# Window attention's product with V: four 32-key groups per head pair replaced by one 64-key group on V and a shifted copy of V

## The chip, the cores and the metric

The kernel runs on one core of a Trainium2 chip. The metric is the device time of one launch in microseconds (us), the median of the runs. Lower is better.

## The reference

The input is 8 sequences of 512 tokens with 128 features. A first layer (linear attention with Taylor features, 16 heads) and a feed-forward transformer of 6 layers follow one another, each with a residual. The change touches the 6 layers only, in the attention over windows. Cut to what matters, for each of 6 layers:

```python
WINDOW, HEADS, DIM_HEAD = 32, 16, 64
qkv = x @ Wqkv                              # 128 -> 3 * 1024
q, k = l2norm(q) * qs, l2norm(k) * ksc      # per head
q = q * cos * scale + rotate_half(q) * sin * scale
k = k * cos * inv + rotate_half(k) * sin * inv
bk2, bv2 = look(bk), look(bv)               # window before + own window: 64 keys for 32 queries
sim = einsum('bhwie,bhwje->bhwij', bq, bk2) * 8
attn = softmax(where(mask, -max, sim), -1)  # 32 x 64 per window and head
out = einsum('bhwij,bhwje->bhwie', attn, bv2)
x = out.reshape(b, n, 1024) @ Wo + x
x = (a * gelu(gate)) @ W2 + b2 + x          # feed-forward, hidden width 341
```

So each block of 32 queries attends to the 64 keys of its own window and the one before it; the first window has no window before it.

## The kernel before

The features stand on the partitions (x is held transposed, 128 x 512 per sequence). A unit u is one sequence in one layer (48 units). A step n is one pair of heads of one unit (8 steps per unit, 384 in all, `NS`); an index m is two steps, that is four heads (192 in all), and the softmax works on one m at a time, in tiles of 128 x 1024.

Every engine runs its own list of stages. All lists come from one table, `PLACE`: stage `X` of step n (or of unit u, with 8u) is put at the place n + PLACE[X], the stages of all steps are sorted by place, and each engine issues its own ones in that order. A place therefore gives the order on an engine; it is no time. Semaphores hold the data dependences across engines. The stages are software-pipelined: the projection of step n stands about 7 steps ahead of its scores, the product with V some 4 steps behind.

The stages in the order in which a head pair goes through them, with lines of the profile (most matmuls are recorded at line 480, the helper `mm`, and are told apart by their tiles):

- PJ (TensorE, `PS<-LH,LXH` and `PS<-LXH,LH` rows are products of this kind, each as three products of high and low parts), PQ (ScalarE, L1177, squares into SX), PT (VectorE, L891: the two rotary products at once, into TPB), TS (SyncE, L445: TPB with neighbouring partitions swapped into TR by DMA), SS (TensorE, `PS<-SX,C`: sums of squares), AD (GpSimd, L1312: TPB + TR into Q or K).
- NM1, NM2, RW, RQ, RB: the inverse norms, by VectorE and ScalarE, written to DRAM (L453) and read back to all partitions as RB (SyncE, L463). PR (GpSimd, L1294) multiplies K by RB.
- S1 (TensorE): the mask product and then 64 small products `PS<-K,Q`, each a 64-row, 32-column piece of the array. It waits for PR of its second step.
- MX (VectorE, L915 and L920), S3 (ScalarE, L1201: 16 exponentials of 128 x 64 into SC), SU (VectorE, L926, L928), NP (GpSimd, L1317: probabilities times 1/sum).
- TT (VectorE, L936, L937): 32 x 32 block transposes; the part for the own window goes to PP[:, 0], that for the window before to PX. PX (SyncE, L470, L471): two DMAs move PX by 32 partitions into PP[:, 1], so that each block of 32 keys has beside it the probabilities of its own queries and of the queries of the next window.
- VP (TensorE) and VC (ScalarE, L1191): V of one 128-token chunk for eight heads, into VV.
- PV (TensorE, `PS<-PP,VV`): for each m four groups of 16 products (rho = 0 to 3). A product has 32 keys on 32 rows of the array, 64 columns of V, and 64 query columns (own and next window) as the moving operand; neighbouring key blocks add into the same PSUM columns, and so rho = 1 to 3 each wait until the group before is done (`pv_pe`). The four groups stand at four places in TensorE's list.
- PVn (ScalarE, L1214): 128 x 1024 from PSUM to AOT. WO and the feed-forward (F1 to F5) follow once per unit.

```python
PLACE = {
    "S1": 0.07, "MX": 0.18, "S3": (0.52, 0.62, 1.38, 1.44), "SU": 1.45, "NP": 1.74, "TT": 2.63, "PX": 2.78,
    "PV": (3.60, 3.67, 4.87, 5.14), "PVn": 5.23, "PJ": (-7.60, -7.06), "PQ": (-7.54, -7.13),
```

A float32 product appears as two MATMUL and two LDWEIGHTS records, so 64 products per m are 128 records, and 192 m make the count of 24576 in the rows.

## Time and profile before

| | |
|---|---|
| median of 3 runs | 3836.64 us (3830.94 to 3848.4) |
| profiled execution | 3838.31 us, its span 3836.5 us |
| TensorE busy | 3549.6 us (93%) |
| VectorE busy | 2627.8 us (68%) |
| ScalarE busy | 2549.0 us (66%) |
| GpSimd busy | 2022.4 us (53%) |
| mean granted TensorE clock | 0.980 |

Busy time is the time in which at least one instruction of the engine ran; since matmuls overlap, TensorE's busy time also counts the tails of small products. Idle time of an engine is put down to whatever released it. The first 670 us or so belong to the first layer, which the change only reorders; the rest is the 6 layers in a steady rhythm.

### The profile page before, as it was taken

To read this page: it belongs to the slowest core of one execution; us is meant where nothing else is said; L and a number is where in the kernel's file an instruction comes from. 1 tells how busy PE (TensorE), PEld (TensorE's weight loads), DVE (VectorE), ACT (ScalarE), POOL (GpSimd) and SP (SyncE) were. 2 spreads that over 40 slices of the span, in tenths; PEclk is the share of its full clock that TensorE was granted. 3 is DMA by queue.
4 is the path that set the end of the run, shared out by engine and by line. 5 is a ranking of instruction groups with operands and counts; after the bars stand their busy time and mean duration, and the time that the engine had idled before them with its cause. 6 is when DMAs were issued, how large, how long until landed. Compare 5 with 4: busy or idle time off the path is not lost.

```text
span 3836.5 us, 149435 instructions
## 1 busy us (share of the span) xinstructions
PE 3549.6 (93%) x65224; PEld 2293.5 (60%) x65416; DVE 2627.8 (68%) x3583; ACT 2549.0 (66%) x5965; POOL 2022.4 (53%) x1564
## 2 busy tenths in 40 slices
PE   7999998799999999999999999999999999999997
PEld 4555554466666666666666666666666666666664
DVE  3555555577777777777776777777777777767662
ACT  4655564476767676777666766777767767677773
POOL 0000000666666666666666666666666666666651
PEclk9999999799999999999999999999999999999997
DMA  1000000333333333333333433333433333433330
GB/s 49 6 6 6 6 6 3 130 129 117 123 125 132 121 124 121 122 130 129 118 121 114 138 123 123 115 124 121 136 117 128 113 132 120 134 113 126 126 109 25
DMA packets 222618, 389.72 MB, mean 102 GB/s; under 512 B 63758, under 2 KB 101900, under 8 KB 221836
## 3 DMA queue, kind: packets, MB, share of 16 engines
q1 hardware_dynamic: 196080, 364.42, 27.5%
q10 hardware_dynamic: 25884, 15.73, 1.4%
q8 instruction: 514, 8.42, 0.9%
q14 instruction: 140, 1.15, 0.1%
HBM read 124.14 MB, written 7.34 MB: 34 GB/s over the span
## 4 chain that ended last, share of the span: by engine, by line
PE 69%; DVE 12%; ACT 7%; issue 5%; DMA 3%; SPq 2%; POOL 1%; ACTq 0%; POOLq 0%; DVEq 0%
PE PS L480 68%; ACT SC L1201 4%; DVE MX L915 2%; DMA RB<-root_scratch 2%; DVE TPB L891 2%; DVE SM L926 2%; DVE PX L937 1%; DMA PP<-PX 1%; POOL K L1294 1%; DVE VAR L958 1%; ACT AOT L1214 1%; DVE H L965 1%; ACT XCH L1072 1%; DVE VAR L956 1%; DVE BQ L920 1%
## 5 line engine op out<-in xcount | busy, mean ns | idle before, releaser
L891 DVE SCALAR_TENSOR_TENSOR TPB<-PS,VEC,C 128x1024 f32<-128x1024 f32 x768 | 961.0, 1263 | 98.4 <-ACT SX L1177 89.2
L1201 ACT ACTIVATE SC<-PS,BQ,RQ 128x64 f32<-128x64 f32 x3072 | 966.2, 430 | 26.0 <-DVE BQ L920 25.6
L1294 POOL TENSOR_TENSOR K<-K,RB 128x512 f32<-128x512 f32 x384 | 492.4, 1282 | 727.2 <-DMA RB<-root_scratch 726.7
L480 PEld LDWEIGHTS PS<-PP,VV 32*64 32x64 f32 x24576 | 436.1, 133 | 314.0 <-issue 210.8
L480 PE MATMUL PS<-PP,VV 32*64 32x64 f32 (+1 forms) x24576 | 542.0, 223 | 72.1 <-ACT AOT L1214 32.9
L1177 ACT ACTIVATE SX<-PS 128x512 f32<-128x512 f32 x768 | 475.5, 628 | 195.0 <-PE PS L480 188.8
L926 DVE TENSOR_REDUCE SM<-SC 128x16 f32<-128x1024 f32 x192 | 234.2, 1220 | 388.7 <-ACT SC L1201 388.6
L1312 POOL TENSOR_TENSOR K<-TPB,TR 128x512 f32<-128x512 f32 x384 | 493.8, 1286 | 0.0
L1312 POOL TENSOR_TENSOR Q<-TPB,TR 128x512 f32<-128x512 f32 x384 | 492.9, 1284 | 0.0
L1317 POOL TENSOR_TENSOR SC<-SC,RC 128x1024 f32<-128x1024 f32 x192 | 366.2, 1907 | 158.1 <-DVE RC L928 154.5
L480 PE MATMUL PS<-LXH,LH 128*128 128x512 f32 x768 | 350.2, 456 | 16.9 <-DVE TPB L891 9.8
L1191 ACT COPY VV<-PS 128x512 f32<-128x512 f32 x384 | 238.3, 620 | 188.6 <-PE PS L480 185.5
L1214 ACT COPY AOT<-PS 128x1024 f32<-128x1024 f32 x192 | 197.3, 1028 | 248.0 <-PE PS L480 246.1
L480 PE MATMUL PS<-AOT,LO 128*128 128x512 f32 x768 | 338.6, 594 | 0.0
L480 PEld LDWEIGHTS PS<-K,Q 64*32 64x32 f32 x24576 | 255.8, 105 | 126.2 <-issue 80.5
L480 PE MATMUL PS<-K,Q 64*32 64x64 f32 (+1 forms) x24576 | 294.1, 225 | 35.0 <-issue 19.4
L480 PE MATMUL PS<-LXH,LL 128*128 128x512 f32 x768 | 305.4, 398 | 0.0
L480 PE MATMUL PS<-LXL,LH 128*128 128x512 f32 x768 | 304.9, 397 | 0.0
L1260 POOL TENSOR_TENSOR XR<-XR,T 128x512 f32<-128x512 f32 x8 | 12.9, 1611 | 524.0 <-DVE T L862 524.0
L480 PE MATMUL PS<-SX,C 128*32 128x128 f32 x6144 | 253.3, 281 | 4.8 <-ACT SX L1177 3.0
L1133 ACT ACTIVATE PA<-PS 128x768 f32<-128x768 f32 (+1 forms) x192 | 169.8, 884 | 128.2 <-PE PS L480 127.1
L915 DVE TENSOR_REDUCE MX<-PS 128x16 f32<-128x1024 f32 x192 | 234.0, 1219 | 25.4 <-PE PS L480 24.7
(166 smaller groups left out, 6076.8 us busy)
## 6 DMA issues: line engine op xcount, KB each, us to landing
TR<-TPB SPq DMA_DIRECT2D x768, 256.0 KB, 2.7
RB<-root_scratch SPq DMA_DIRECT2D x768, 128.0 KB
PP<-PX SPq DMA_DIRECT2D x192, 192.0 KB, 2.6
WS<-in_wqkv ACTq DMA_DIRECT2D x72, 128.0 KB, 2.5
PP<-PX SPq DMA_DIRECT2D x192, 48.0 KB, 2.3
root_scratch<-NV SPq DMA_DIRECT2D x384, 8.0 KB
LO<-in_wo ACTq DMA_DIRECT2D x6, 512.0 KB, 4.6
T<-in_x SPq DMA_DIRECT2D x8, 256.0 KB, 3.0
```

Source lines behind the costliest of these rows:

```text
L480: return e.matmul(dst, lhsT, rhs, start=start, stop=stop, **kw)
L891: e.scalar_tensor_tensor(TPB[:, n % 3:4 + n % 2:3 + n % 2 - n % 3, w, :], g, VEC[:, l, 9 + w:10 + w], C[:, at:at + 1024].rearrange("p (o c ...
L915: e.tensor_reduce(MX[:, :], g, AX_X, ALU.max).then_inc(sem["s1_dve"], 1)
L926: e.tensor_reduce(SM[:, :], SC[m % 2][:, :, :, :].rearrange("p g x k -> p g (x k)"), AX_X, ALU.add).then_inc(sem["su_dve"], 1)
L1133: e.activation(P[t % 3][:, :, 0:n], PS[:, 2 * (t % 2):2 * (t % 2) + 2, 0:n], ACT.Square, bias=1.0, scale=0.25).then_inc(sem["as_act"], 1)
L1177: e.activation(SX[i % 3][:, :], bk("PJ", key)[:, :], ACT.Square).then_inc(sem["pj_act"], 1)
L1191: e.copy(VV[:, c, 512 * hf:512 * hf + 512], bk("VP", key)[:, :]).then_inc(sem["vp_act"], 1)
L1201: p = e.activation(SC[m % 2][:, g, :, :].rearrange("p x k -> p (x k)"), bank[s][:, at:at + 64], ACT.Exp, bias=BQ[m % 2][:, g:g + 1], scale ...
L1214: e.copy(AOT[:, 2 * p % 8:2 * p % 8 + 2, :], PS[:, 2:4, :]).then_inc(sem["pv_act"], 1)
L1294: e.tensor_tensor(dst, dst, RB[n % 2][:, :], ALU.mult).then_inc(sem["pr_pool"], 1)
L1312: e.tensor_tensor((Q, K)[w][:, n % 8, :], TPB[:, n % 3, w, :], TR[n % 2][:, w, :], ALU.add).then_inc(sem["ad_pool"], 1)
L1317: e.tensor_tensor(sc, sc, RC[m % 2][:, :].rearrange("p (g o) -> p g o", o=1).broadcast_to([128, 16, 64]), ALU.mult).then_inc(sem["np_pool" ...
```

## The change

- The products of PV are cut another way. For each block of 32 queries one product takes all 64 keys at once: 64 rows of the array, 64 columns of V, 32 moving columns. Nothing is added up in PSUM any more, so the three waits within PV go, and PV becomes one stage of 64 products in one piece (place 4.641).
- For odd blocks the 64 keys are an aligned half of a chunk of VV. For even blocks they straddle such halves, so there is a second copy of V, VS, shifted by 32 tokens. It is made by two DMAs per half unit from VV (stage VS), issued from ScalarE's queue.
- Both transposes of TT now write PP; the half of the probabilities that sits on the wrong 32 partitions is exchanged: GpSimd copies all of PP to PX (new stage PC, 128 x 1024), and four DMAs of 32 partitions bring the pieces back into PP (stage PX on SyncE, before two DMAs). PX waits for PC alone.
- PVn writes AOT in another order of its columns. Q, K and TPB become one tensor QK: PT writes its first product straight into the slot of Q or K, AD adds in place, and PT takes over the wait for a free slot.
- All numbers of PLACE are new. Of the table the diff shows the lines of the stages spoken of; further ones: RB from -2.15 to -2.314, PR from -1.83 to -1.300, AD from -5.68 to -5.235, RQ from -1.78 to -1.149.

The diff, without the remaining lines of the table and without the places where only a name changes:

```diff
@@ -26,17 +26,18 @@
...
-    "S1": 0.07, "MX": 0.18, "S3": (0.52, 0.62, 1.38, 1.44), "SU": 1.45, "NP": 1.74, "TT": 2.63, "PX": 2.78,
-    "PV": (3.60, 3.67, 4.87, 5.14), "PVn": 5.23, "PJ": (-7.60, -7.06), "PQ": (-7.54, -7.13),
...
+    "S1": 0.063, "MX": 0.247, "S3": (0.668, 0.831, 0.849, 1.249), "SU": 1.650, "NP": 1.797, "TT": 2.880,
+    "PC": 3.194, "PX": 3.300, "PV": 4.641, "PVn": 5.989, "VS": (2.322, 5.841), "PJ": (-7.624, -7.175),
...
@@ -235,6 +236,8 @@
         for j in range(8):
             at(z + j + P["VP"], group, "VP", 8 * u + j, "vp_act", 8 * u + j + 1)
             at(z + j + P["VC"], o.put, "VC", 8 * u + j)
+        for i in range(2):
+            at(z + P["VS"][i], o.put, "VS", u, i)
         at(z + P["WO"], group, "WO", u, "wo_dve", 2 * u + 2)
         at(z + P["F1"], group, "F1", u, "f1_act", 2 * u + 2)
         at(z + P["F2"], group, "F2", u, "f2_dve", 4 * u + 1)
@@ -265,11 +268,10 @@
             at(n + P["RQ"], group, "RQ", n // 4, "rq_act", n // 4 + 1)
         if n % 2 == 0:
             m = n // 2
-            for st in ("S1", "MX", "SU", "NP", "TT", "PX", "PVn"):
+            for st in ("S1", "MX", "SU", "NP", "TT", "PC", "PX", "PV", "PVn"):
                 at(n + P[st], o.put, st, m)
             for i in range(4):
                 at(n + P["S3"][i], o.put, "S3", m, i)
-                at(n + P["PV"][i], o.put, "PV", m, i)
     for b in range(NB):
         z = 8 * (NB * (DEPTH - 1) + b)
         at(z + P["E1"], o.put, "E1", b)
@@ -324,11 +326,10 @@
         W2 = sb("W2", [128, 3, 128])
         LX = [(sb(f"LXH{i}", [128, L], F32R), sb(f"LXL{i}", [128, L], F32R)) for i in range(2)]
         BI = [sb(f"BI{i}", [128, 8]) for i in range(2)]
-        Q = sb("Q", [128, 8, L])
-        K = sb("K", [128, 8, L])
+        QK = sb("QK", [128, 10, 2, L])
         VV = sb("VV", [128, 4, 1024])
+        VS = sb("VS", [128, 4, 1024])
         AOT = sb("AOT", [128, 8, L])
-        TPB = sb("TPB", [128, 5, 2, L])
         TR = [sb(f"TR{i}", [128, 2, L]) for i in range(2)]
         EU = sb("EU", [128, L])
         ER = sb("ER", [128, L])
@@ -337,7 +338,7 @@
         SX = [sb(f"SX{i}", [128, L]) for i in range(3)]
         SC = [sb(f"SC{i}", [128, 16, 2, 32]) for i in range(2)]
         PP = [sb(f"PP{i}", [128, 2, 16, 32]) for i in range(2)]
-        PX = sb("PX", [128, 16, 32])
+        PX = sb("PX", [128, 2, 16, 32])
         MX = sb("MX", [128, 16])
         BQ = [sb(f"BQ{i}", [128, 16]) for i in range(2)]
         RQ = [sb(f"RQ{i}", [128, 2, 16]) for i in range(2)]
@@ -463,13 +464,11 @@
                         e.dma_start(RB[n % 2][64 * s:64 * s + 64, :], r.broadcast_to([64, L])).then_inc(sem[f"rb_in{n % 2}"], 16)
                 elif st == "PX":
                     m, = key
-                    a, z = PX, PP[m % 2]
-                    if m > 1:
-                        on.wait_ge("pv_pe", 4 * m - 4)
-                    on.wait_ge("tt_dve", 2 * m + 2)
-                    e.dma_start(z[0:96, 1, :, :], a[32:128, :, :]).then_inc(sem[f"px_in{m % 2}"], 16)
-                    e.dma_start(z[96:128, 1, :, :].rearrange("p (x c) a -> p x c a", c=4)[:, :, 0:3, :],
-                                a[0:32, :, :].rearrange("p (x c) a -> p x c a", c=4)[:, :, 1:4, :]).then_inc(sem[f"px_in{m % 2}"], 16)
+                    z = PP[m % 2]
+                    on.wait_ge("pc_pool", m + 1)
+                    for r in range(4):
+                        x, to = 1 - r % 2, 32 * (r + 1 - 2 * (r % 2))
+                        e.dma_start(z[to:to + 32, 1 - x, :, :], PX[32 * r:32 * r + 32, x, :, :]).then_inc(sem[f"px_in{m % 2}"], 16)
             for b in range(NB):
                 on.wait_ge(f"y_out{b}", 16)
                 on.wait_ge(f"x1_out{b}", 16)
@@ -676,27 +675,23 @@
                     free(on, st, key)
                     e.transpose(bk(st, key)[:, 0:128], NV[:, 2, :], ident).then_inc(sem["rq_pe"], 1)
                 elif st == "PV":
-                    p, rho = key
+                    p, = key
                     u, half = p // 4, p % 4 // 2
-                    if rho == 0:
-                        on.wait_ge("vp_act", 8 * u + 4 * half + 4)
-                        on.wait_ge(f"px_in{p % 2}", 32 * (p // 2) + 32)
-                        on.wait_ge("tt_dve", 2 * p + 1)
-                        if p:
-                            on.wait_ge("pv_act", p)
-                    else:
-                        on.wait_ge("pv_pe", 4 * p + rho)
-                    for c in range(4):
-                        for x in range(2):
-                            for s in range(2):
-                                r = (rho + 2 * x + s) % 4
-                                j = 4 * c + r
-                                w = min(2, 16 - j)
-                                h = 2 * ((2 * p + x) % 8) + s
-                                y = mm(bank[2 + x][64 * s:64 * s + 64, 32 * j:32 * j + 32 * w],
-                                       VV[32 * r:32 * r + 32, c, 64 * h:64 * h + 64],
-                                       PP[p % 2][32 * r:32 * r + 32, 0:w, 8 * s + 4 * x + c, :],
-                                       rho == 0 and c == 0, rho == 3 and c == 3, skip_group_check=True)
+                    on.wait_ge("vp_act", 8 * u + 4 * half + 4)
+                    on.wait_ge(f"vs_in{half}", 32 * u + 32)
+                    on.wait_ge(f"px_in{p % 2}", 64 * (p // 2) + 64)
+                    on.wait_ge("tt_dve", 2 * p + 2)
+                    if p:
+                        on.wait_ge("pv_act", p)
+                    for x in range(2):
+                        for c in range(4):
+                            for w in range(2):
+                                for a in range(2):
+                                    for s in range(2):
+                                        h, at = 2 * ((2 * p + x) % 8) + s, 256 * x + 64 * c + 32 * w
+                                        y = mm(bank[2 + a][64 * s:64 * s + 64, at:at + 32],
+                                               (VS, VV)[w][64 * a:64 * a + 64, c, 64 * h:64 * h + 64],
+                                               PP[p % 2][64 * a:64 * a + 64, w, 8 * s + 4 * x + c, :], skip_group_check=True)
                     y.then_inc(sem["pv_pe"], 1)
                 elif st == "WO":
                     u, = key
@@ -884,11 +879,11 @@
                     at = CONST["tab"][0] + 1024 * w
                     if n > 1:
                         on.wait_ge(f"t3_in{n % 2}", 32 * (n // 2))
-                    if n > 2:
-                        on.wait_ge("ad_pool", 2 * n - 4)
+                    if n > 7:
+                        on.wait_ge("s1_pe", n // 2 - 3)
                     on.wait_ge("pj_act", i + 1)
                     g = bk("PJ", key).rearrange("p (o c) -> p o c", o=1).broadcast_to([128, 2, 512])
-                    e.scalar_tensor_tensor(TPB[:, n % 3:4 + n % 2:3 + n % 2 - n % 3, w, :], g, VEC[:, l, 9 + w:10 + w],
+                    e.scalar_tensor_tensor(QK[:, n % 8:9 + n % 2:8 + n % 2 - n % 8, w, :], g, VEC[:, l, 9 + w:10 + w],
                                            C[:, at:at + 1024].rearrange("p (o c) -> p o c", o=2), ALU.mult,
                                            ALU.mult).then_inc(sem["pj_dve"], 1)
                 elif st == "NM1":
@@ -928,13 +923,11 @@
                     e.reciprocal(RC[m % 2][:, :], SM[:, :]).then_inc(sem["su_dve"], 1)
                 elif st == "TT":
                     m, = key
-                    if m:
-                        on.wait_ge(f"px_in{(m - 1) % 2}", 32 * ((m - 1) // 2) + 32)
                     if m > 1:
-                        on.wait_ge("pv_pe", 4 * m - 4)
+                        on.wait_ge("pv_pe", m - 1)
                     on.wait_ge("np_pool", m + 1)
-                    e.transpose(PP[m % 2][:, 0, :, :], SC[m % 2][:, :, 1, :]).then_inc(sem["tt_dve"], 1)
-                    e.transpose(PX[:, :, :], SC[m % 2][:, :, 0, :]).then_inc(sem["tt_dve"], 1)
+                    e.transpose(PP[m % 2][:, 0, :, :], SC[m % 2][:, :, 0, :]).then_inc(sem["tt_dve"], 1)
+                    e.transpose(PP[m % 2][:, 1, :, :], SC[m % 2][:, :, 1, :]).then_inc(sem["tt_dve"], 1)
                 elif st == "WO":
                     u, = key
                     l, b = lb(u)
@@ -1186,7 +1179,7 @@
                     j, = key
                     u, hf, c = j // 8, j // 4 % 2, j % 4
                     if u:
-                        on.wait_ge("pv_pe", 16 * u - 8 + 8 * hf)
+                        on.wait_ge("pv_pe", 4 * u - 2 + 2 * hf)
                     on.wait_ge("vp_pe", j + 1)
                     e.copy(VV[:, c, 512 * hf:512 * hf + 512], bk("VP", key)[:, :]).then_inc(sem["vp_act"], 1)
                 elif st == "S3":
@@ -1206,12 +1199,21 @@
                     on.wait_ge("rq_pe", q + 1)
                     e.copy(RQ[q % 2][:, :, :].rearrange("p y (i c) -> p (y i) c", c=4),
                            bk(st, key)[:, 0:128].rearrange("p (c i) -> p i c", c=4)[:, 0:8, :]).then_inc(sem["rq_act"], 1)
+                elif st == "VS":
+                    u, hf = key
+                    c = slice(512 * hf, 512 * hf + 512)
+                    if u == 0 and hf == 0:
+                        on.wait_ge("vs_pool", 1)
+                    on.wait_ge("vp_act", 8 * u + 4 * hf + 4)
+                    e.dma_start(VS[32:128, :, c], VV[0:96, :, c]).then_inc(sem[f"vs_in{hf}"], 16)
+                    e.dma_start(VS[0:32, 1:4, c], VV[96:128, 0:3, c]).then_inc(sem[f"vs_in{hf}"], 16)
                 elif st == "PVn":
                     p, = key
                     if p > 3:
                         on.wait_ge("wo_pe", p // 4)
-                    on.wait_ge("pv_pe", 4 * p + 4)
-                    e.copy(AOT[:, 2 * p % 8:2 * p % 8 + 2, :], PS[:, 2:4, :]).then_inc(sem["pv_act"], 1)
+                    on.wait_ge("pv_pe", p + 1)
+                    y = AOT[:, 2 * p % 8:2 * p % 8 + 2, :].rearrange("p x (c a w) -> p a (x c) w", a=2, w=64)
+                    e.copy(y, PS[:, 2:4, :].rearrange("p a (c w) -> p a c w", w=64)).then_inc(sem["pv_act"], 1)
                 elif st == "F1":
                     u, = key
                     if u:
@@ -1305,11 +1307,20 @@
                 elif st == "AD":
                     i, = key
                     n, w = i // 2, i % 2
-                    if n > 7:
-                        on.wait_ge("s1_pe", n // 2 - 3)
                     on.wait_ge("pj_dve", i + 1)
                     on.wait_ge(f"t3_in{n % 2}", 32 * (n // 2) + 32)
-                    e.tensor_tensor((Q, K)[w][:, n % 8, :], TPB[:, n % 3, w, :], TR[n % 2][:, w, :], ALU.add).then_inc(sem["ad_pool"], 1)
+                    e.tensor_tensor(QK[:, n % 8, w, :], QK[:, n % 8, w, :], TR[n % 2][:, w, :], ALU.add).then_inc(sem["ad_pool"], 1)
+                elif st == "PC":
+                    m, = key
+                    if m:
+                        on.wait_ge(f"px_in{(m - 1) % 2}", 64 * ((m - 1) // 2) + 64)
+                    on.wait_ge("tt_dve", 2 * m + 2)
+                    e.tensor_copy(PX[:, :, :, :], PP[m % 2][:, :, :, :]).then_inc(sem["pc_pool"], 1)
+                elif st == "LO" and key[0] == 0:
+                    on.wait_ge("xa_dve", 16)
+                    for b in range(NB):
+                        on.wait_ge(f"x1_out{b}", 16)
+                    e.memset(VS[0:32, 0, :], 0.0).then_inc(sem["vs_pool"], 1)
                 elif st == "NP":
                     m, = key
                     on.wait_ge("su_dve", 2 * m + 2)
```

What the engines issue. First TensorE, in the stretch between two S1 of one unit, before the change (`PS<-PP,VV` is PV, `PS<-SX,C` is SS, the rows with LXH and LXL are PJ and VP):

```order
L480 MATMUL PS<-SX,C 32x128 x8
L480 MATMUL PS<-PP,VV 64x64 x13
L480 MATMUL PS<-PP,VV 64x32
L480 MATMUL PS<-PP,VV 64x64 x2
L480 MATMUL PS<-LXH,LH 128x512
L480 MATMUL PS<-LXL,LH 128x512
L480 MATMUL PS<-LXH,LL 128x512
L480 MATMUL PS<-AOT,LO 128x512 x8
L480 MATMUL PS<-PP,VV 64x64 x12
```

The same kind of stretch with the change:

```order
L479 MATMUL PS<-SX,C 32x128 x8
L479 MATMUL PS<-PP,VS 64x32 x4
L479 MATMUL PS<-PP,VV 64x32 x4
...
L479 MATMUL PS<-PP,VS 64x32 x4
L479 MATMUL PS<-PP,VV 64x32 x4
L479 MATMUL PS<-LH,LXH 128x512
L479 MATMUL PS<-LL,LXH 128x512
L479 MATMUL PS<-LH,LXL 128x512
```

The four groups of PV, with wide products between them, are now one group of 16 fours; SS stands ahead of it as before.

SyncE's queue over one m, before (L470 and L471 bring PX into PP, L463 is RB, L445 is TS):

```order
L445 DMA TR<-TPB 64x1024 [waits pj_dve,ad_pool]
L445 DMA TR<-TPB 64x1024
L470 DMA PP<-PX 96x512 [waits tt_dve,pv_pe]
L471 DMA PP<-PX 32x4x96
L463 DMA RB<-root_scratch 64x512 [waits pr_pool]
L463 DMA RB<-root_scratch 64x512
```

and with the change:

```order
L446 DMA TR<-QK 64x1024
L471 DMA PP<-PX 32x512 [waits pc_pool]
L471 DMA PP<-PX 32x512 x3
L464 DMA RB<-root_scratch 64x512 [waits pr_pool]
L464 DMA RB<-root_scratch 64x512
L446 DMA TR<-QK 64x1024 [waits pj_dve,ad_pool]
```

The two transfers of PP have become four, at the same spot of the queue, and what they wait for is GpSimd's copy instead of VectorE's transposes.

GpSimd's list with the change (L1318 is the new copy, L1296 is PR, L1312 is AD, L1328 is NP):

```order
L1296 TENSOR_TENSOR QK<-QK,RB 128x512 [waits rb_in0,ad_pool]
L1312 TENSOR_TENSOR QK<-QK,TR 128x512 [waits t3_in0,pj_dve]
L1312 TENSOR_TENSOR QK<-QK,TR 128x512 [waits pj_dve]
L1318 COPY PX<-PP 128x1024 [waits tt_dve,px_in0]
L1296 TENSOR_TENSOR QK<-QK,RB 128x512 [waits rb_in1,ad_pool]
L1312 TENSOR_TENSOR QK<-QK,TR 128x512 [waits t3_in1,pj_dve]
L1312 TENSOR_TENSOR QK<-QK,TR 128x512 [waits pj_dve]
L1328 TENSOR_TENSOR SC<-SC,RC 128x1024 [waits su_dve]
```

The copy stands just ahead of the PR of an odd step; before, that list had the same rows without it.

## Rows read from the trace of the kernel before

**Rows 1.** The page: busy us (share of the span) and instructions.

```profile
PE 3549.6 (93%) x65224; PEld 2293.5 (60%) x65416; DVE 2627.8 (68%) x3583; ACT 2549.0 (66%) x5965; POOL 2022.4 (53%) x1564
```

**Rows 2.** Windows of one steady stretch: length, busy time per engine (instructions), clock, DMA.

```profile
1690.00:2200.00 510.00, 474.49 (x10318) 319.31 (x10351) 375.99 (x482) 358.16 (x885) 330.86 (x255) 1.00 0.36 123
```

**Rows 3.** The page's groups: busy, mean ns | idle before, and what ended it.

```profile
L480 PE MATMUL PS<-PP,VV 32*64 32x64 f32 (+1 forms) x24576 | 542.0, 223 | 72.1 <-ACT AOT L1214 32.9
L480 PE MATMUL PS<-K,Q 64*32 64x64 f32 (+1 forms) x24576 | 294.1, 225 | 35.0 <-issue 19.4
```

**Rows 4.** Timeline of TensorE: start us, duration us of the merged run, group.

```profile
2001.19 0.64 PE L480 MATMUL PS<-SX,C 128*32 128x128 f32 x16
2001.76 0.69 PE L480 MATMUL PS<-PP,VV 32*64 32x64 f32 x32
2002.39 0.50 PE L480 MATMUL PS<-LXH,LH 128*128 128x512 f32 x1
2002.72 0.39 PE L480 MATMUL PS<-LXL,LH 128*128 128x512 f32 x1
2002.95 0.40 PE L480 MATMUL PS<-LXH,LL 128*128 128x512 f32 x1
2003.28 0.69 PE L480 MATMUL PS<-PP,VV 32*64 32x64 f32 x32
2003.90 0.50 PE L480 MATMUL PS<-LH,LXH 128*128 128x512 f32 x1
```

**Rows 5.** Timeline of TensorE at one S1, with its weight loads (PEld).

```profile
2009.78 1.30 PEld L480 LDWEIGHTS PS<-K,Q 64*32 64x32 f32 x128 [0.61 <-POOL K L1294]
2009.79 1.46 PE L480 MATMUL PS<-K,Q 64*32 64x32 f32 x128
2011.18 0.50 PE L480 MATMUL PS<-LH,LXH 128*128 128x512 f32 x1
```

**Rows 6.** The page's groups of weight loads.

```profile
L480 PEld LDWEIGHTS PS<-PP,VV 32*64 32x64 f32 x24576 | 436.1, 133 | 314.0 <-issue 210.8
L480 PEld LDWEIGHTS PS<-K,Q 64*32 64x32 f32 x24576 | 255.8, 105 | 126.2 <-issue 80.5
```

**Rows 7.** Waits: who waited for whom, us in total, times, longest us.

```profile
POOL K L1294 <- DMA RB<-root_scratch: 726.7, 203, 10.0
PE PS L480 <- DVE TPB L891: 65.8, 63, 1.3
PE PS L480 <- POOL K L1294: 14.7, 21, 3.2
```

**Rows 8.** Chain that ended last, 2003.95 to 2009.79: start us, us, what.

```profile
2003.95 1.28 SPq L463
2005.29 3.03 DMA RB<-root_scratch
2008.45 1.29 POOL K L1294
2009.79 3.61 PE PS L480 x97
```

**Rows 9.** GpSimd's groups; ScalarE's DMA issues: ns min/median/max, first to last us.

```profile
L1250 POOL COPY AO<-VA 128x256 f32<-128x256 f32 x6 | 2.3, 439 | 6.9 <-DMA VA<-in_awq 6.9
L1317 POOL TENSOR_TENSOR SC<-SC,RC 128x1024 f32<-128x1024 f32 x192 | 366.2, 1907 | 158.1 <-DVE RC L928 154.5 <-DMA RB<-root_scratch 3.6
L1019 ACTq DMA_DIRECT2D WS<-in_wqkv x72: 334/374/1957, 685.2 to 3222.4; - x72
```

**Rows 10.** The page's DMA issues: KB each, us to landing; and queue q1.

```profile
q1 hardware_dynamic: 196080, 364.42, 27.5%
PP<-PX SPq DMA_DIRECT2D x192, 192.0 KB, 2.6
PP<-PX SPq DMA_DIRECT2D x192, 48.0 KB, 2.3
LO<-in_wo ACTq DMA_DIRECT2D x6, 512.0 KB, 4.6
```

11 lines of the change are left out of this document (4 added, 7 removed), and 16 rows, old and new, of the table PLACE.

## The prediction

> **What bounds the kernel now.** I read the busy shares first: TensorE 93%, VectorE 68%, ScalarE 66%, GpSimd 53% [rows 1]. The share is the same within the steady part: of 510 us TensorE is busy in 474.5, VectorE in 376, ScalarE in 358, GpSimd in 331, at a granted clock of 1.00 (2.4 GHz) [rows 2]. So TensorE sets the pace, and 7% of the time it waits. The six layers take about 3836.5 - 670 = 3166 us for 384 steps, 8.2 us per step and 16.5 us per m (two steps).
>
> The product with V is the costliest group on TensorE by busy time, 542.0 us, or 2.8 us per m, and TensorE is idle for another 72.1 us just ahead of it, 32.9 of them until ScalarE has copied the last result to AOT [rows 3]. The waits put 726.7 us on GpSimd for RB, which costs little in itself: TensorE waits only 14.7 us for that K, against 65.8 us for VectorE's TPB, which frees a PSUM bank [rows 7]. In the chain a piece shows how RB gets on the path: 1.28 us to issue two DMAs, 3.03 until RB lands, 1.29 for PR, then TensorE [rows 8].
>
> **What PV costs now.** In the timeline one of its four groups of 32 records starts at 2001.76 and the next product at 2002.39, 0.63 us later; another takes 2003.28 to 2003.90, 0.62 [rows 4]. The merged run lasts 0.69 us, of which the last record's own length is 0.22 (the mean of rows 3), so that the 32 starts take 0.47 us, 15 ns per record; the other 0.16 us is the start-up and the end of a group. Coming out of wide products costs 0.10 more: 2002.95 to 2003.28 is 0.33 where the wide products stand 0.23 apart [rows 4]. I count that for two of four groups, since some stand behind SS, which has small tiles too. Per m: 4 x 0.63 + 2 x 0.10 = 2.7 us.
>
> **What it costs with the change.** There are again 64 products, 128 records. Each moves 32 columns where it moved 64, and still loads 64 columns of V. What a load takes I read from two groups: 133 ns with 64 columns, 105 ns with 32 [rows 6]. 28 ns for 32 columns is 56 ns for 64, and with four pieces of the array side by side one record per 14 ns. That is the 15 ns of the trace: the present groups already run at the rate of their loads, and halving the moving columns gains nothing by itself. I take 15 ns again: 128 x 0.015 = 1.9 us, one start and end 0.16, together 2.05 us. The gain per m is 0.65 to 0.7 us, and it consists of three start-ups and ends and of the entries; 0.68 x 192 = **131 us**. The three waits inside PV go with them.
>
> The bounds of the 15 ns. Below: S1, the nearest row with half the columns per load, needs (1.46 - 0.22) / 128 = 10 ns per record [rows 5]; PV would take 1.4 us and the gain be 1.3 x 192 = 250 us. Above: the change has in each four products two on the same 64 rows that differ only in their columns of the array, where before all four had rows of their own. If two such loads took turns, 64 loads of 56 ns would follow one another, 3.6 us, 3.75 with the ends, a loss of 1.05 x 192 = 200 us. S1 excludes most of it: it has four column pieces on the same rows, and its 64 loads of 28 ns per half would take 1.8 us in turn, where its starts take 1.24. So I stay at 15 ns, to which the present PV is nearest.
>
> A rule of the Trainium skill speaks against this step: "TensorE: Matmul & The Clock Gate", section "Part 3: Packing small matmuls — row/col tiling", says that a weight load overlaps matmuls in flight only where its row group is another one. S1's row disagrees, as far as it goes; by the rule the sum would be some 200 us higher than before instead of 152 lower. The same page, section "Wait — 56ns, not 53.3ns?", puts the distance between matmul starts at no less than about 25 ns however few columns move; by that estimate 128 records need 3.2 us and the change would lose. The 15 and 10 ns per record of the trace disagree with it for pieces side by side.
>
> **TensorE's waits.** PV stood 0.82 of a step behind PX (3.60 and 2.78) and now stands 1.34 behind (4.641 and 3.300); PVn stood 0.37 of a step ahead of the next PV and now 0.65 (5.989 against 6.641). Both sources of the 72.1 us get more room, about 4 us and 2 us. I count half of the 72: 36 us. The RB that TensorE waited for through K: RB and PR were 0.32 of a step apart and are now 1.01, 8.3 us, against 1.28 + 3.03 us of issue and landing [rows 8]; the 14.7 us go. What is late next is VectorE: TensorE comes 0.68 us earlier per m to the same PT that frees its banks, and I let the 65.8 us grow by 30. Together 36 + 15 - 30 = **21 us**.
>
> **Costed at nothing, and what hides it.**
> - GpSimd's copy of 1024 elements per partition. The nearest rows are 439 ns for a copy of 256, so up to 1.76 us, and 1.91 us for the two-input operation on 1024 [rows 9]; below, nothing excludes 1 us. At 1.8 us per m it adds 345 us, and GpSimd goes from 65% to 76% of the steady time. Its 727 us of waiting for RB hold it. Were it on the path, its whole price would be 192 x 1.8.
> - ScalarE's DMAs: 192 issues, with its weight DMAs as the nearest row at 0.37 us [rows 9] and SyncE's at 0.64 [rows 8]: 70 to 125 us on an engine with 30% of idle time, plus a short wait for its own last copy of V. Squares, exponentials and AOT queue behind it. Cover: 1.3 us, twice in 65 us.
> - SyncE's four DMAs in place of two: 2.6 us in place of 1.3, ahead of RB in the same queue, and the queue now stops until GpSimd has made its copy. RB and TS stand behind it. The cover is the step between RB and PR and the 1.7 steps between TS and AD; without it 1.3 us per m would reach TensorE, 250 us.
> - Traffic: VS is 960 KB per half unit, 96 times 0.98 MB, 94 MB beside 364 MB that now take 27.5% of the DMA engines [rows 10], so 7 points more. For one such burst I take 5 to 9 us from the 512 KB in 4.6 us [rows 10]; PV stands 2.3 steps, 19 us, behind it. PX's own transfers (2.3 and 2.6 us before [rows 10]) may land a few us later if they meet it.
> - PVn's new column order, AD in place, the wait that PT takes over (PJ of that step stands behind S1 on TensorE already): nothing. TT writes as much as before. The first layer is only reordered: within 10 us either way.
>
> **The sum.** 3838 (the profiled execution, 1.7 us above the median) - 131 - 21 = **3686 us**, 4% faster. TensorE would be busy less and the clock stays as it is.
>
> **Rivals.**
> - *The gain is swallowed by new waits.* PV's chain is longer by a copy and two issues, SyncE's queue stops for GpSimd, VectorE and ScalarE have all their work still, and every place is new. For it: VectorE would be at 78% and ScalarE at 75% with lists as rigid as before, and the 65.8 us show that VectorE is already the nearest. Against it: each wait that I can place has gained room. If two thirds of the 152 us come back as waits for banks or K: about 3785 us, from 3740 to 3835.
> - *Loads on the same rows take turns.* PV then takes 3.75 us in place of 2.7 per m; the place is every run of four products `VS`, `VV`, and it decides from 21 ns per record on (2.7 us over 128), above which PV costs more than before. 3838 + 200 - 36 (waits ahead of PV) = about 4000 us. This is the other side. Against it stands S1. The section "Part 3" of the Trainium skill's page "TensorE: Matmul & The Clock Gate" would have it so.
> - *PV runs at S1's rate.* If not the columns loaded but something else made the 15 ns, 128 records take 1.24 us: 3838 - 250 - 21 + 30 (more waiting for VectorE) = about 3600 us. For it: half the moving columns. Against it: the load groups of 133 and 105 ns.
>
> **How the numbers follow.** The forecast gets 0.64 and its own range is 3640 to 3740; swallowed 0.18; turns 0.10; S1's rate 0.08. The range of 8 in 10 is 3600 to 3800: it leaves out the turns, a part of the swallowed case and a part of the fastest. A measurement of this kernel can tell about 0.5%, 19 us, from no change. Faster by more than that are the forecast, the fastest case and six tenths of the swallowed one, 0.83; within it 0.06; slower 0.11, the turns and a little for waits that cost more than PV gains.
>
> **What would show it.** Right: one merged run of 128 records `PS<-PP,VS` and `PS<-PP,VV` per m, 2.0 to 2.2 us long, 15 ns per record; TensorE's busy time down by 130 us or so; its idle time ahead of PV below 40 us; GpSimd's wait for RB cut to a small part and its new copy at 1 to 1.8 us; TensorE's wait for K near nothing, that for TPB near 100 us. Wrong: 20 ns per record or more (turns), 10 (S1's rate), or TensorE idle for more than 290 us in all with PV at its 2.1 us (swallowed), and then the waits name the engine.

## The result

The changed kernel is slower: 4253.0 us (median of 4 runs, 4241.9 to 4259.6) against 3838.6 for the kernel before beside it (3830.9 to 3848.4). The ratio is 1.1075, with a 95% interval of 1.1038 to 1.1112. The prediction was 3686 us, range 3600 to 3800. The profiled execution took 4257.3 us with a span of 4255.5, so 419 us more than the span of before, 3836.5.

The page of the changed kernel: busy shares, the granted clock in 40 slices, two queues.

```profile
PE 3713.0 (87%) x65416; PEld 2427.8 (57%) x65416; DVE 2742.6 (64%) x3583; ACT 2563.5 (60%) x5965; POOL 2214.5 (52%) x1757
...
PEclk9999997899999999999999889999999999999997
...
q10 hardware_dynamic: 75036, 110.12, 10.5%
q8 instruction: 514, 8.42, 0.9%
```

All shares are lower than in [rows 1], since every engine waits more. Busy time is another matter: TensorE is busy for 163 us more, and idle for 4255.5 - 3713.0 = 542 us, where it was idle for 287. Its mean granted clock over the span fell from 0.980 to 0.925. With the two levels of 1.2 and 2.4 GHz that is 2 x (1 - 0.925) x 4255 = 638 us at the lower one, the half level, against 153 before. In two windows of the steady part it shows as 0.94 and 0.91 where it had been 1.00 in both (the first is in [rows 2]), and the DMA share went from 0.36 to 0.47:

```profile
1690.00:2200.00 510.00, 442.15 (x9085) 298.47 (x9083) 350.25 (x425) 318.17 (x782) 321.55 (x254) 0.94 0.47 138
2200.00:2720.00 520.00, 453.97 (x9281) 310.70 (x9281) 351.63 (x429) 321.17 (x789) 324.09 (x256) 0.91 0.47 137
```

The page's groups of the changed kernel, as in [rows 3, 6, 9]:

```profile
L479 PE MATMUL PS<-PP,VS 64*64 64x32 f32 x12288 | 435.3, 228 | 125.5 <-issue 122.2
L479 PE MATMUL PS<-PP,VV 64*64 64x32 f32 x12288 | 438.0, 228 | 117.4 <-issue 117.2
L479 PE MATMUL PS<-LXH,LH 128*128 128x512 f32 x768 | 407.3, 530 | 55.4 <-DVE QK L886 32.5
L886 DVE SCALAR_TENSOR_TENSOR QK<-PS,VEC,C 128x1024 f32<-128x1024 f32 x768 | 974.9, 1270 | 710.8 <-ACT SX L1170 691.8
```

and the group of the kernel before that answers to the third:

```profile
L480 PE MATMUL PS<-LXH,LH 128*128 128x512 f32 x768 | 350.2, 456 | 16.9 <-DVE TPB L891 9.8
```

The two halves of PV run at the same time, so their busy times don't add. Taken together (the window of the whole span, instructions that read PP alone) TensorE is busy with PV for 476.6 us, where it was 542.0. But it stops inside PV for 125.5 + 117.4 = 243 us, and 239 of them the profile puts down to "issue": it waited for nothing that the profile knows. Before, the idle time at PV was 72.1 us, and most of it stood ahead of PV [rows 3].

**Where the 419 us are.** PV with its idle time: 476.6 + 242.9 = 719.5 us now, 542.0 + 72.1 = 614.1 before, so +105. Everything else that TensorE does: 3713.0 - 476.6 = 3236.4 us busy against 3549.6 - 542.0 = 3007.6, so +229, for almost the same instructions. Other idle time: 542.5 - 242.9 = 299.6 against 286.9 - 72.1 = 214.8, so +85. The sum is 419. The +229 fit the clock: 485 us more are spent at the half level, and if TensorE worked through all of them, half, some 240 us, would be lost. That is an upper bound, since TensorE is idle in a part of this time: f5_vs_apart below has 585 us more at the half level, and TensorE's whole busy time is only 128 us longer. The wide product LXH x LH takes 530 ns in the mean where it took 456, but that mean is no measure of the clock: in e1_split it is 461, with more time at the half level.

TensorE's timeline at one PV (start us, duration us of the merged run, group):

```profile
2486.22 0.65 PE L479 MATMUL PS<-SX,C 128*32 128x128 f32 x16
2486.80 0.32 PE L479 MATMUL PS<-PP,VS 64*64 64x32 f32 x8
...
2487.75 0.30 PE L479 MATMUL PS<-PP,VS 64*64 64x32 f32 x8
2487.87 0.28 PE L479 MATMUL PS<-PP,VV 64*64 64x32 f32 x2
2489.07 0.25 PE L479 MATMUL PS<-PP,VV 64*64 64x32 f32 x3 [0.92 <-issue]
...
2490.01 0.50 PE L479 MATMUL PS<-LH,LXH 128*128 128x512 f32 x1
```

Eight records start every 0.12 us, 15 ns per record, as forecast. At 2487.87, after 74 of the 128, it stops for 1.2 us, and then goes on at the old rate. Without the stop this PV would take 2.0 us; it takes 3.2.

Waits of the changed kernel, with two of [rows 7] in the last two rows:

```profile
ACT SX L1170 <- PE PS L479: 596.4, 478, 6.5
PE PS L479 <- issue: 288.2, 202, 7.0
POOL QK L1296 <- DMA RB<-root_scratch: 261.3, 114, 4.8
PE PS L479 <- DVE QK L886: 50.4, 81, 1.6
```

TensorE's waits for VectorE (50.4 us, before 65.8) and for GpSimd (27.3, before 14.7) stayed small. In the changed kernel ScalarE and, behind it, VectorE wait for a late TensorE.

The new transfers on ScalarE's queue: DMA issues (KB each, us to landing), and how long ScalarE takes to issue the second of them (ns min/median/max; the first takes 636 in the median).

```profile
VS<-VV ACTq DMA_DIRECT2D x96, 768.0 KB, 7.0
VS<-VV ACTq DMA_DIRECT2D x96, 192.0 KB, 8.5
L1209 ACTq DMA_DIRECT2D VS<-VV x96: 642/662/3132, 735.9 to 4170.5; - x96
```

### The profile page after: what moved, and what is told of

It is laid out like the page before. It is cut to its first block, busy times and chain, and to the rows that moved or that the text cites. A ratio compares the mean times of both kernels' runs of the same rounds, so it can differ in the third digit from the quotient of the medians.

```text
span 4255.5 us, 150597 instructions
## 1 busy us (share of the span) xinstructions
PE 3713.0 (87%) x65416; PEld 2427.8 (57%) x65416; DVE 2742.6 (64%) x3583; ACT 2563.5 (60%) x5965; POOL 2214.5 (52%) x1757
## 3 DMA queue, kind: packets, MB, share of 16 engines
q8 instruction: 514, 8.42, 0.9%
## 4 chain that ended last, share of the span: by engine, by line
PE 68%; issue 9%; ACT 9%; DVE 5%; DMA 4%; POOL 2%; SPq 2%; ACTq 0%; POOLq 0%; DVEq 0%
PE PS L479 68%; ACT SC L1194 4%; DMA RB<-root_scratch 4%; ACT SX L1170 2%; DVE QK L886 2%; POOL QK L1296 1%; ACT VV L1184 1%; SPq L464 1%; SPq L446 1%; ACT L979 1%; DVE SM L921 0%; SPq L471 0%; POOL XCL L1306 0%; POOL SC L1328 0%; POOL QK L1312 0%
## 5 line engine op out<-in xcount | busy, mean ns | idle before, releaser
L886 DVE SCALAR_TENSOR_TENSOR QK<-PS,VEC,C 128x1024 f32<-128x1024 f32 x768 | 974.9, 1270 | 710.8 <-ACT SX L1170 691.8
L1312 POOL TENSOR_TENSOR QK<-QK,TR 128x512 f32<-128x512 f32 x768 | 967.2, 1281 | 0.0
L1296 POOL TENSOR_TENSOR QK<-QK,RB 128x512 f32<-128x512 f32 x384 | 490.7, 1278 | 261.3 <-DMA RB<-root_scratch 261.3
L1328 POOL TENSOR_TENSOR SC<-SC,RC 128x1024 f32<-128x1024 f32 x192 | 365.6, 1904 | 438.9 <-DVE RC L923 438.9
L479 PE MATMUL PS<-PP,VS 64*64 64x32 f32 x12288 | 435.3, 228 | 125.5 <-issue 122.2
L479 PE MATMUL PS<-PP,VV 64*64 64x32 f32 x12288 | 438.0, 228 | 117.4 <-issue 117.2
L479 PEld LDWEIGHTS PS<-PP,VS 64*64 64x64 f32 x12288 | 379.8, 142 | 168.3 <-issue 164.7
L479 PEld LDWEIGHTS PS<-PP,VV 64*64 64x64 f32 x12288 | 388.1, 144 | 131.1 <-issue 130.8
L1318 POOL COPY PX<-PP 128x1024 f32<-128x1024 f32 x192 | 199.2, 1037 | 315.8 <-DVE PP L930 315.5
L479 PEld LDWEIGHTS PS<-QK 64*32 64x32 f32 x24576 | 274.3, 108 | 117.3 <-issue 73.3
L479 PE MATMUL PS<-QK 64*32 64x64 f32 (+1 forms) x24576 | 309.3, 231 | 28.7 <-POOL QK L1296 27.3
L479 PE MATMUL PS<-SX,C 128*32 128x128 f32 x6144 | 261.1, 286 | 17.7 <-issue 14.7
```

The costliest lines, as they stand in the source:

```text
L479: return e.matmul(dst, lhsT, rhs, start=start, stop=stop, **kw)
L886: e.scalar_tensor_tensor(QK[:, n % 8:9 + n % 2:8 + n % 2 - n % 8, w, :], g, VEC[:, l, 9 + w:10 + w], C[:, at:at + 1024].rearrange("p (o c) ...
L1296: e.tensor_tensor(dst, dst, RB[n % 2][:, :], ALU.mult).then_inc(sem["pr_pool"], 1)
L1312: e.tensor_tensor(QK[:, n % 8, w, :], QK[:, n % 8, w, :], TR[n % 2][:, w, :], ALU.add).then_inc(sem["ad_pool"], 1)
L1318: e.tensor_copy(PX[:, :, :, :], PP[m % 2][:, :, :, :]).then_inc(sem["pc_pool"], 1)
L1328: e.tensor_tensor(sc, sc, RC[m % 2][:, :].rearrange("p (g o) -> p g o", o=1).broadcast_to([128, 16, 64]), ALU.mult).then_inc(sem["np_pool" ...
```

## The experiments

My theories after the result were these. **Instructions**: TensorE's instructions reach it in pieces by DMA (queue q8: 514 packets, 8.42 MB in all in both kernels, so 16 KB each), and PV uses 256 instructions in 1.9 us, right behind S1, which uses 256 in 1.3 us; supply falls behind. **Clock**: new stops, or the new form itself, lower the granted clock. **Traffic**: VS's transfers delay instructions and inputs. **Places**: the new table of places, with PV in one piece, makes banks and inputs late. **GpSimd and SyncE**: the copy, and the queue that stops for it.

The runs, with medians, ratio to the kernel before on the same chip, idle time of TensorE (span less busy) and time at the half level (from the mean clock, as above):

| run | us | ratio (95%) | idle, us | half level, us |
|---|---|---|---|---|
| before, as profiled | 3838.6 | 1 | 287 | 153 |
| changed | 4253.0 | 1.1075 (1.1038 to 1.1112) | 542 | 638 |
| e1_split | 4254.9 | 1.1098 (1.1082 to 1.1115) | 529 | 672 |
| e2_one | 4235.2 | 1.1046 (1.1027 to 1.1064) | 566 | 665 |
| e3_novs | 3980.3 | 1.0377 (1.0344 to 1.0410) | 417 | 327 |
| e4_bmerged | 4134.3 | 1.0782 (1.0766 to 1.0798) | 459 | 396 |
| e6_groups | 4299.6 | 1.1222 (1.1199 to 1.1245) | 502 | 689 |
| e7_vschunks | 4227.8 | 1.1030 (1.0998 to 1.1061) | 526 | 457 |
| e8_novs_groups | 4076.5 | 1.0648 (1.0628 to 1.0668) | 399 | 383 |
| e10_warm | 4218.1 | 1.1018 (1.0997 to 1.1038) | 480 | 371 |
| b2_copy | 3834.8 | 1.0013 (1.0004 to 1.0023) | 290 | 138 |
| b3_rb | 3841.1 | 1.0022 (1.0009 to 1.0036) | 294 | 154 |
| f1_split_novs | 4075.5 | 1.0646 (1.0604 to 1.0687) | 432 | 407 |
| f2_split_px | 4304.8 | 1.1204 (1.1142 to 1.1265) | 568 | 733 |
| f3_stop | 4120.4 | 1.0750 (1.0730 to 1.0770) | 479 | 453 |
| f4_vs | 4250.2 | 1.1080 (1.1064 to 1.1097) | 537 | 654 |
| f5_vs_apart | 4404.8 | 1.1490 (1.1460 to 1.1520) | 717 | 738 |
| f6_apart | 4347.2 | 1.1331 (1.1300 to 1.1361) | 621 | 731 |

m1_bursts and m2_forms are kernels of their own, and are told by their windows.

### Is it the table of places?

**e1_split**: the changed kernel's operations with the old table, PV in four groups of 32 records.

```
-    "PC": 3.194, "PX": 3.300, "PV": 4.641, "PVn": 5.989, "VS": (2.322, 5.841), ...
+    "TT": 2.63, "PX": 3.05, "PC": 2.75, "VS": (2.46, 6.46), "PV": (4.2, 4.67, 4.87, 5.14), "PVn": 5.23, ...
-                    p, = key
+                    p, i = key
...
+                    x = i // 2
+                    for c in range(2 * (i % 2), 2 * (i % 2) + 2):
```

> The changed kernel with the table of places of before (PC 2.75, PX 3.05 and VS 2.46, 6.46 added) and PV in four groups of 16 products at the places 4.20, 4.67, 4.87, 5.14, with no wait between them; same products, same transfers. Theory F (TensorE's instructions arrive no faster than about one packet of 256 per few us, and PV in one piece uses up 256 within 1.9 us): the idle time put down to issue ahead of PV falls from 240 us to under 40, and the time comes to 3750 to 3900 us. Theory C (the transfers of VS slow all other transfers, the instruction packets among them): the idle time within PV stays above 150 us, since VS is still moved, and the time stays above 4050. Theory T (the new table of places is what costs): as F in time, but then the next run with PV in one piece is as fast as this one.

**e2_one**: the same table with PV whole.

```
-    "PV": (4.2, 4.67, 4.87, 5.14), "PVn": 5.23,
+    "PV": 4.87, "PVn": 5.23,
```

> As the run before, with the table of places of before, but PV in one piece at 4.87. It differs from that run by the splitting alone. F: idle time for issue at PV above 150 us and 100 to 350 us slower than the split one, 4000 to 4250. T: within 40 us of the split one. C: both near 4200.

4254.9 and 4235.2 us: with the old places the change costs the same, in four groups or in one. So neither the new table by itself nor PV in one piece by itself is what loses the time, and three expectations missed: the instruction theory's 3750 to 3900 for the split run and its 100 to 350 us between the two, and the theory of places, which had both there. The traffic theory had its time (above 4050) but not its stops (above 150 us in the split run). But the idle time isn't at the same spots. The groups of e1_split, and behind them those of e2_one:

```profile
L479 PE MATMUL PS<-PP,VS 64*64 64x32 f32 x12288 | 431.7, 228 | 27.2 <-issue 23.1
L479 PE MATMUL PS<-PP,VV 64*64 64x32 f32 x12288 | 420.5, 224 | 22.9 <-issue 22.8
L479 PE MATMUL PS<-XCH,W1H 128*128 128x512 f32 x288 | 170.7, 593 | 162.7 <-ACT VV L1185 69.1 <-POOL XCL L1307 47.7 <-DVE QK L887 45.8
L478 PE MATMUL PS<-PP,VV 64*64 64x32 f32 x12288 | 391.6, 221 | 51.3 <-issue 51.1
L478 PE MATMUL PS<-PP,VS 64*64 64x32 f32 x12288 | 392.6, 222 | 21.0 <-issue 20.8
```

Inside PV e1_split stops for 50 us instead of 243, but 163 us stand ahead of the first product of the layer's end (58 before), and the clock is as low as ever (0.921). e2_one has PV whole, 128 records in a row as in the changed kernel, and stops for only 51.3 + 21.0 = 72 us. Its PV stands 0.80 of a step behind S1 (4.87 and 4.07), that of the changed kernel 0.58 (4.641 and 4.063), and V's products (VP, at -0.60) lie in between, which stand behind PV in the changed kernel. So a run of 128 isn't enough for the stops; how near S1 it stands counts too (the sections "near" and "far" below test that alone). And stops inside PV are one form of the loss, and not all of it: TensorE is idle for 529 and 566 us in these two runs, 542 in the changed kernel.

**e4_bmerged**: the kernel before, with all four groups of the old PV at one place.

```
-    "PV": (3.60, 3.67, 4.87, 5.14), "PVn": 5.23,
+    "PV": (4.870, 4.871, 4.872, 4.873), "PVn": 5.23,
```

> The kernel before with its four PV groups next to each other (places 4.870 to 4.873) and nothing else changed; it has no VS, no copy on GpSimd and the old table. F: stalls for issue at PV, 10 us before, rise to over 100 us and the time to 3950 to 4150. C and T: within 1.5% of before, 3780 to 3895, a part of the mode changes between groups being saved.

4134.3 us, 1.078: to bring the *old* product together late costs 300 us. The time is in the instruction theory's range, but the stops that it asked for (over 100 us) aren't there: the groups have 66.2 us of idle time, 14.5 by issue. What is late is ScalarE, for whose copies of V TensorE waits 125.8 us, and the layer's end:

```profile
L480 PE MATMUL PS<-PP,VV 32*64 32x64 f32 (+1 forms) x24576 | 544.3, 223 | 66.2 <-issue 14.5
L480 PE MATMUL PS<-XCH,W1H 128*128 128x512 f32 x288 | 168.8, 586 | 154.4 <-ACT VV L1191 69.9 <-DVE TPB L891 48.1 <-POOL XCL L1304 36.2
```

The old table starts PV's first half at 3.60, behind a chain without a copy; the change makes PV one step at 4.641, and gives this up. The forecast counted one run in place of four as a gain of start-ups alone.

### How much is V's shifted copy?

**e3_novs**: the changed kernel without VS's transfers and the wait for them; PV reads VV in place of VS, so that the shifted copy is left out and half of the products are formed with unshifted V.

```
-                    on.wait_ge(f"vs_in{half}", 32 * u + 32)
...
-                    (VS, VV)[w][64 * a:64 * a + 64, c, 64 * h:64 * h + 64],
+                    (VV, VV)[w][64 * a:64 * a + 64, c, 64 * h:64 * h + 64],
...
-                    e.dma_start(VS[32:128, :, c], VV[0:96, :, c]).then_inc(sem[f"vs_in{hf}"], 16)
-                    e.dma_start(VS[0:32, 1:4, c], VV[96:128, 0:3, c]).then_inc(sem[f"vs_in{hf}"], 16)
```

> The changed kernel without the DMAs of VS and without the wait for them; PV reads VV in place of VS (that part of the computation is left out, the even query blocks get the wrong keys). C: the stalls within PV fall from 240 us to under 60 and the time to 3950 or less. F: they stay above 150 us and the time above 4130, a little below 4253 since each packet has less traffic beside it.

3980.3 us: the two DMAs per half unit cost 273 us of the 414, all that comes with them taken together. Between the two profiled executions the span differs by 263 us: TensorE has 126 us less of idle time and 138 less of busy time. The clock is at 0.959, and the stops inside PV are about half, between the two expectations (under 60 and over 150):

```profile
L479 PE MATMUL PS<-PP,VV 64*64 64x32 f32 x24576 | 443.0, 222 | 132.9 <-issue 124.3
```

What is left, 3980 against 3838, is all the rest of the change, and PV still stops for 124 us by issue. Even free of VS's cost the change would lose 3.8%.

**e7_vschunks**: VS moved in seven smaller transfers per half unit, each right behind the copy of V that it reads.

```
+        for j in range(8):
+            at(z + j + P["VC"] + 0.02, o.put, "VS", u, j)
...
+                    e.dma_start(VS[32:128, cc, c], VV[0:96, cc, c]).then_inc(sem[f"vs_in{hf}"], 16)
+                    if cc < 3:
+                        e.dma_start(VS[0:32, cc + 1, c], VV[96:128, cc, c]).then_inc(sem[f"vs_in{hf}"], 16)
```

> The changed kernel with VS moved in 8 pieces per unit of 192 and 64 KB, each right behind the copy of its chunk of V, in place of 2 of 960 KB: the same bytes, spread out. C as bursts: stalls within PV fall to about the 125 us of the run without VS, time near 3990 to 4080. C as mere amount of traffic: no change within 1%. F alone: no change.

4227.8 us, a ratio of 1.1030 whose interval overlaps that of the changed kernel, with stops of 73.8 + 65.5 = 139 us inside PV instead of 243 and 457 us at the half level instead of 638. Both fell, the stops nearly to those of e3_novs as the theory of bursts had it, but its 3990 to 4080 us did not come; ScalarE issues 672 DMAs here in place of 192, at 0.52 us each for most of them, and they may have taken back what was gained (no run tells).

**f6_apart**: the changed kernel with the two halves' transfers 1.5 steps apart instead of 0.5.

```
-    "PVn": 5.989, "VS": (2.322, 5.841),
+    "PVn": 5.989, "VS": (3.322, 5.841),
```

> The changed kernel with the first half's transfers at 3.322 of a step instead of 2.322, so that the two halves' bursts lie 1.5 steps apart instead of 0.5. If bursts on top of one another delay instructions and inputs most, 4150 us or less; if it is the amount of traffic or the time to use it, within 30 us of 4253.

4347.2 us, slower. PV's idle time grew to 235.3 + 99.3 us, and the profile says issue again, but here the row of VS's second transfer names TensorE among those who waited for its landing, 123.4 us in 37 times, which it doesn't in the changed kernel:

```profile
  PE PS L479: 123.4, 37
```

In the stretch from 1690 to 2720 us, 13 waits, 43 us in all, stand ahead of PV's first record, about one for each unit; in the changed kernel none does. The stops behind the first record are 62 us there, against 68. So the run lost by PV waiting for a copy that was issued 1.3 steps ahead of it; bursts that lie apart took little from the stops inside PV.

### Traffic and queue in the kernel before

**f4_vs**: the kernel before, with VS's transfers from ScalarE's queue (they write buffers that nothing reads, in 38 of 48 units), and PV waiting for them.

```
+                elif st == "VS":
+                    on.wait_ge("vp_act", 8 * u + 4 * hf + 4)
+                    if u or hf:
+                        on.wait_ge(f"vs_in{1 - hf}", 112 * (u + hf))
+                    for i in range(4):
+                        e.dma_start((EU, ER, EX, ES)[i][32:128, :], VV[0:96, i, c]).then_inc(sem[f"vs_in{hf}"], 16)
+                        if i < 3:
+                            e.dma_start((EU, ER, EX, ES)[i + 1][0:32, :], VV[96:128, i, c]).then_inc(sem[f"vs_in{hf}"], 16)
```

> The kernel before with the changed kernel's extra traffic from ScalarE's queue (the same DMAs of V to shifted rows, 192 and 64 KB in seven pieces per half unit, at the same places, in 38 of the 48 units; what they write is read by nothing), and the old PV waiting for them as the new one does. Theory (traffic matters by delaying instructions where they are used fast): the old PV uses its instructions slower, so little is stalled inside it; the traffic costs some 50 to 150 us, 3900 to 3980. Rival, the traffic costs by itself what it cost with the new PV (273 us): 4050 or more (4110 less a fifth that is left out). Rival, traffic is harmless in the old form: 3850 or less.

4250.2 us, as slow as the changed kernel. But the old PV isn't stopped by issue; ScalarE is. Its waits, and the length of one of its seven issues:

```profile
ACT SX L1181 <- issue: 252.5, 47, 6.2
ACT LXH L1070 <- issue: 147.6, 29, 6.2
L1220 ACTq DMA_DIRECT2D ER<-VV x76: 534/618/2037, 744.4 to 3517.2; - x76
```

252.5 + 147.6 = 400 us over 76 bursts is 5.3 us for each: seven issues of 0.6 us, 4.3 us, and the wait that I had added for the other half's landing. So this run shows what ScalarE's issues and that wait cost the kernel, not what traffic costs it.

**f5_vs_apart**: f4_vs with the first half's burst one step later, so that ScalarE doesn't wait for a landing.

```
-    "PX": 2.78, "VS": (2.46, 6.46),
+    "PX": 2.78, "VS": (3.46, 6.46),
```

> f4_vs with one half's transfers a whole step later (place 3.46 instead of 2.46): the two halves no longer fall on the same moment, so that ScalarE does not wait for the first half's landing before it can issue the second's, which in f4_vs stood as 252 us of idle time ahead of SX. The traffic is the same. Theory now: most of f4_vs's loss was ScalarE's stop, and the traffic by itself costs the old kernel little, 3850 to 3920 us. Rival: the traffic costs by itself, through late inputs, instructions and the clock, what it costs the changed kernel: 4050 us or more.

4404.8 us, and again not a measurement of traffic: the first group of PV, at 3.60, now waits for the burst at 3.46.

```profile
PE PS L482 <- DMA ES<-VV: 356.0, 38, 10.6
```

38 waits of 9.4 us. Neither theory is tested by it. What DMA traffic alone costs, without issues on ScalarE, stays open for the whole kernel; m1_bursts below has it for TensorE alone.

**b2_copy**: the kernel before with GpSimd's copy of 128x1024 in each m, read by nothing. **b3_rb**: the kernel before with RB 0.3 of a step earlier. **f3_stop**: b2_copy with the copy at 2.70 in place of 2.90, and SyncE's transfers PX waiting for it.

```
+                elif st == "PC":
+                    on.wait_ge("tt_dve", 2 * m + 2)
+                    e.tensor_copy(PY[...], SC[m % 2][...]).then_inc(sem["pc_pool"], 1)
```

```
-    "RQ": -1.78, "RB": -2.15, "PR": -1.83,
+    "RQ": -1.78, "RB": -2.45, "PR": -1.83,
```

```
                     on.wait_ge("tt_dve", 2 * m + 2)
+                    on.wait_ge("pc_pool", m + 1)
                     e.dma_start(z[0:96 ...
```

> The kernel before with one more copy of 128x1024 on GpSimd per m, of the probabilities, which nobody reads, at 2.90 in its list, behind the transposes. The work of GpSimd hides it: within 1% of before, 3800 to 3870. A rival that the copy delays K and Q for TensorE: 3900 or more.

> The kernel before with the transfers of RB 0.3 of a step earlier in SyncE's list (-2.45 in place of -2.15), nothing else. If the RB in the chain is worth anything, 10 to 40 us faster than before; if the norms are not ready there, SyncE stops for them and TR comes late: slower by as much.

> The kernel before with GpSimd's copy of 128 x 1024 at place 2.70 of each step, and SyncE's transfers PX waiting for it, where the copy alone cost nothing (1.001). Nothing else is changed. Theory (the stop is harmless): 3835 us within 20. Rival: the stop on SyncE's queue is a good part of the loss: 3900 us or more, with idle time for TR's and RB's landings.

The copy itself is free, 1.0013 with GpSimd at 58%, and so is an earlier RB, 1.0022. But the copy in the chain from PX to PP costs 287 us (1.075). PV's group in f3_stop:

```profile
L482 PE MATMUL PS<-PP,VV 32*64 32x64 f32 (+1 forms) x24576 | 578.5, 234 | 289.7 <-DMA PP<-PX 282.3
```

It is PV that waits, 282 us for PX's landing, 1.47 us per m: the copy's 1.05 us and what GpSimd is behind when it gets there. (The copy stands at another place than in b2_copy, so a part may be its own order on GpSimd.) The first group of the old PV had almost no room behind PX; one more link of 1 us is paid in full. I had sought a rival's stop of RB and TR behind SyncE's wait, and the rows name PP.

**f1_split_novs** and **f2_split_px** ask the same of e1_split, since there PV has room:

```
-                    on.wait_ge(f"vs_in{half}", 32 * u + 32)
...
-                    e.dma_start(VS[32:128, :, c], VV[0:96, :, c]).then_inc(sem[f"vs_in{hf}"], 16)
-                    e.dma_start(VS[0:32, 1:4, c], VV[96:128, 0:3, c]).then_inc(sem[f"vs_in{hf}"], 16)
```

```
-    "TT": 2.63, "PX": 3.05, "PC": 2.75,
+    "TT": 2.63, "PX": 3.35, "PC": 2.75,
```

> The table of e1_split (the new product in four groups at the old places, GpSimd's copy), but V is not copied: PV reads V itself in place of the shifted copy, which leaves that part of the result out and all of the traffic on ScalarE's queue. Theory: the traffic costs what it cost in the changed kernel (4253 against 3980, 273 us), through late instructions and through the clock; here then 4255 - 270 = 3985 us, between 3930 and 4050, stretches at the half clock near 330 us. Rival, the four transfers of each PX which wait for GpSimd's copy on SyncE's queue, and the inputs behind them: at or above 4180 us, with idle time of VectorE and TensorE for XCH and LXH as in e1_split. Rival, traffic alone and nothing else: 3860 us or less.

> e1_split with the table's place of PX 0.30 of a step later, so that GpSimd's copy is over when SyncE's queue comes to it. Theory (instructions and clock): no difference, 4255 us within 30. Rival, SyncE's stop for the copy: the stop goes, with up to 0.5 us per step, 4255 - 96 = 4160 us or less, and less idle time for XCH and LXH. Slower than 4285 would say that the swapped halves now come too late for PV.

f1_split_novs gives 4075.5 us, 179 less than e1_split (273 less in e3_novs against the changed kernel). It keeps 132 us ahead of XCH (e1_split 163, e4_bmerged 154). So the late placing seen in e4_bmerged is in it too, and VS takes a smaller part here. The 4075.5 lie just above the range of that expectation, 3930 to 4050. f2_split_px gives 4304.8, 50 us more than e1_split, and its PV now waits 37.2 us for PX. The later place shortened SyncE's stop for the copy from 930 to 595 us and gained nothing. In the changed kernel itself SyncE stops for the copy only 5 times, 33.1 us in all, so there this stop is no cause.

### Instructions and clock

**m1_bursts** (a kernel of its own with TensorE alone at work): A is the new PV twelve times in a row, 64 products each; B is one PV and 12 wide products, 24 times; C the same work with 3 wide products behind each 16; then B and C with VS's transfers always under way, then without again.

```
                    if kind == "B":
                        for x in range(2):
                            part(x, range(4))
                        p = wide(12)
                    else:
                        for x in range(2):
                            for c in (0, 2):
                                part(x, (c, c + 1))
                                p = wide(3)
```

> A kernel of its own (it computes nothing of the reference) that measures the disputed cost by itself. TensorE alone runs sections, each after 40 wide products: A, 768 products of PV's form back to back (12 times 256 instructions); B, 24 rounds of 64 such products in one piece and then 12 wide ones; C, the same products with 3 wide ones behind every 16. Then B and C with a 960 KB transfer of VS's form always in flight, then B and C without it again. Theory F: A runs at the 15 ns per record only for its first few hundred instructions and then stalls for issue, 256 instructions taking clearly more than 1.9 us, 3 to 6; B has stalls within PV where C has next to none, so that B is longer than C by more than 5% in spite of fewer mode changes. Theory C: without traffic B and C have no stalls, and A keeps 1.9 us per 256; with traffic both stall. If neither has stalls, what made them in the whole kernel is open.

Windows of m1_bursts (TensorE busy, loads, clock, DMA share): A, B, C, B with traffic, C with traffic.

```profile
27.34:90.40 63.06, 59.38 (x1625) 54.46 (x1625) 0.00 (x0) 0.00 (x0) 0.75 0.07 27
90.40:216.60 126.20, 126.20 (x3389) 105.32 (x3388) 0.00 (x0) 0.00 (x0) 0.99 0.02 4
216.60:370.80 154.20, 154.20 (x3417) 109.27 (x3409) 0.00 (x0) 0.00 (x0) 1.00 0.01 3
370.80:510.70 139.90, 132.36 (x3398) 109.13 (x3391) 0.00 (x0) 0.00 (x0) 0.96 0.40 102
510.70:666.20 155.50, 154.70 (x3417) 109.58 (x3409) 0.00 (x0) 0.00 (x0) 1.00 0.36 91
```

Three readings. The splitting in four costs (154.2 - 126.2) / (24 x 3) = 0.39 us for each further change from wide to small products (0.41 in the two sections at the end). Traffic at a DMA share of 0.40 makes the compact form 11% slower (139.9 against 126.2), with 7.5 us of idle time and the clock at 0.96, and the spread form 0.8%. And the new PV back to back has a clock of 0.75 in the window, the lead-in at full clock included; there are stops of 1.0 and 1.7 us before the clock falls. So A does stop for issue, as the instruction theory asked, but B without traffic doesn't, and isn't longer than C but 18% shorter: 12 wide products behind every 64 small ones are enough for the instructions to come.

**m2_forms** sets the forms side by side, TensorE alone: twelve times the new PV; twelve times the old; twelve times S1; then the new PV with 2, 4 and 6 wide products behind each, 16 times.

```
            ("new", "N", 12, 0), ("old", "O", 12, 0), ("s1", "S", 12, 0),
            ("n2", "NWW", 16, 0), ("n4", "NWWWW", 16, 0), ("n6", "NWWWWWW", 16, 0),
            ("near", "SWWWN" + 21 * "W", 16, 0), ("far", "S" + 12 * "W" + "N" + 12 * "W", 16, 0),
```

> A kernel of its own again, TensorE alone, no transfers at first. Theory K: stretches of small products by themselves bring TensorE's granted clock down to its half level, without any idle time. Then the sections of 12 x 64 products in a row of PV's new form, of the old form and of S1's form all run at half clock for most of their length; with 2 wide products behind every 64 of the new form still so, with 6 no longer; and 64 of S1's form with 64 of the new form 3 wide ones apart (as the changed kernel has them) show half clock where the same ones 12 apart do not. If the pure sections of old form and S1 stay at full clock and only the new form does not, the new form itself is what costs. If near and far both stay at full clock, the half clock of the whole kernel came from its idle time. With VS's transfers always in flight, near should have more idle time than far if bursts of instructions and traffic together make the stalls.

Windows of m2_forms in this order:

```profile
48.00:89.00 41.00, 38.21 (x1536) 37.56 (x1536) 0.00 (x0) 0.00 (x0) 0.58 0.02 4
102.00:143.90 41.90, 36.00 (x1537) 28.27 (x1536) 0.00 (x0) 0.00 (x0) 1.00 0.02 4
153.80:195.00 41.20, 22.79 (x1523) 20.28 (x1528) 0.00 (x0) 0.00 (x0) 0.58 0.02 4
206.40:269.80 63.40, 59.78 (x2078) 50.59 (x2078) 0.00 (x0) 0.00 (x0) 0.70 0.02 4
283.20:340.00 56.80, 53.09 (x2108) 43.98 (x2108) 0.00 (x0) 0.00 (x0) 1.00 0.02 5
```

The 12 x 256 instructions of three quite different forms all need 41 to 42 us. In rows of the timelines of the three sections, new, old and S1:

```profile
53.49 0.24 PE L80 MATMUL PS<-PP,VV 64*64 64x32 f32 x1 [1.33 <-issue]
118.09 6.86 PE L96 MATMUL PS<-PP,VV 32*64 32x64 f32 x256 [0.59 <-issue]
161.25 2.05 PE L106 MATMUL PS<-VS,VV 64*32 64x64 f32 x128 [1.97 <-issue]
```

S1 shows the supply bare: it works through 256 instructions in 2.1 us or less, stops for 1.4 to 2.0, and from one stop to the next there are 3.66 us in the mean. The other two lie near that by their own pace as well: the old form, since in this kernel too each group of 16 waits for the one before, takes 6.86 us per 512 and then stops for 0.3 to 0.6; the new form at half clock starts a record every 26.5 ns, 3.4 us per 256. So the like totals are in part chance, but all three stop for issue.

What they stop for can be read from the transfers of queue q8 in the traces. A packet holds 256 instructions: there are 172 packets for 44048 records in m1_bursts, 264 for 67704 in m2_forms, and e10_warm, whose program has 1536 instructions more than the changed kernel's, has 520 instead of 514. In the three sections the packets land 3.66, 3.68 and 3.68 us apart in the median. And in the changed kernel, of 152 stops of 0.3 us or more at PV, 151 end between 1.15 and 1.75 us after a packet has landed; only 8% of TensorE's instructions start in that interval. They hold 236.5 of 239.2 us. In e3_novs it is 114 of 117. So the stops inside PV are waits for the next packet of instructions. They aren't a matter of the highest rate alone: the packet that ends such a stop in the changed kernel lands 8.9 us in the median behind the one before, far more than 3.7. It comes too late for S1 and PV together, and what decides when it is fetched no run here shows. The old PV came in four groups of 64 instructions with wide products between.

The second reading is the clock.

```profile
52.00:53.50 1.50, 0.17 (x12) 0.06 (x6) 0.00 (x0) 0.00 (x0) 1.00 0.00 0
54.50:55.00 0.50, 0.50 (x33) 0.50 (x30) 0.00 (x0) 0.00 (x0) 0.54 0.14 33
76.00:80.00 4.00, 4.00 (x158) 4.00 (x156) 0.00 (x0) 0.00 (x0) 0.50 0.01 4
```

The new form in a row goes at 0.58: the clock falls at 54.5 us, one us behind the stop of 1.33, and then stays at half although TensorE hardly stops any more (4.00 of 4.00 us). The old form keeps 1.00, against the expectation, with stops of up to 0.6 us. With two wide products behind each 64 of the new form it is 0.70, and the fall comes behind stops of 0.5 to 1.1 us; with four it is 1.00, with stops of 0.7 us at most, and then the section with *more* work takes less time, 56.8 us against 63.4.

It is tempting to read from this that the new form lowers the clock without any stop. These sections don't show that, as each has stops ahead of its fall. Light work can do it: in the first layer, which the change only reorders, the clock falls seven times in either kernel in or right behind a run of products of four columns, with 0.4 us of idle time at most (at 120 us of the kernel before TensorE is busy in 4.00 of 4.00 us on either side, and the clock goes from 1.00 to 0.54). But in the six layers, where the loss is, each of the 89 falls of the changed kernel from 700 to 3700 us has at least 0.85 us of idle time of TensorE in the few us before it (not each such stop brings a fall), and so have all 16 falls of the two kernels with TensorE alone, 1.1 us or more. The table says the same by run: idle time and time at the half level go up and down together, and the *old* PV, with nothing of the new form, has 453 us at the half level in f3_stop, 654 in f4_vs and 738 in f5_vs_apart, once waits of other kinds make TensorE idle. So a stop costs its own time and some time at the half level behind it. What part the lighter form adds to that stays open.

The sections "near" and "far", with 24 wide products per round, set S1 and the new PV next to each other or apart:

```profile
420.50:578.00 157.50, 149.16 (x4457) 121.68 (x4456) 0.00 (x0) 0.00 (x0) 0.99 0.01 4
592.90:739.00 146.10, 145.93 (x4458) 119.70 (x4460) 0.00 (x0) 0.00 (x0) 1.00 0.02 4
751.90:924.00 172.10, 154.28 (x4451) 125.25 (x4454) 0.00 (x0) 0.00 (x0) 0.96 0.39 98
939.00:1107.00 168.00, 153.54 (x4444) 123.98 (x4444) 0.00 (x0) 0.00 (x0) 0.97 0.39 100
```

The first two, the same work without traffic: 157.5 us with 8.3 idle near, 146.1 with 0.2 apart. The last two, with VS's transfers under way: 172.1 and 168.0, idle 17.8 and 14.5. Two bursts close together cost 0.7 us per round by lack of instructions, and traffic costs 0.9 us or more per round, apart too. Near and far both keep nearly the full clock without traffic, and the expectation had said what that would mean: the half clock of the whole kernel came from its idle time.

**e10_warm**: the changed kernel with four more wide products (bf16, their result overwritten) ahead of each PV.

```
+                    for x in range(4):
+                        mm(bank[2][:, :], identb[:, :], maskb[:, :], skip_group_check=True)
```

> The changed kernel with four more wide bf16 products (mask times identity, overwritten by PV) ahead of PV's 64: 0.9 us more work per m, 170 us in all. K: time at half clock falls from 642 us by more than 150, and the time stays within 60 us of 4253 or falls, since the added work is paid by the clock; the four also give the instructions time to arrive, so stalls within PV fall. If the clock is a consequence of other waits, the time rises by 100 to 170 us.

4218.1 us: with 768 more products on the busiest engine the kernel isn't slower but about 0.5% faster (1.1018 against 1.1075; the intervals just touch at 1.1038). The half level falls from 638 to 371 us and the stops in PV from 243 to 71.2 + 56.7 = 128. It is a small gain, and the time at the half level fell by more than the forecast 150 us. The four products give the instructions time to arrive, and the work is done in time that was idle before.

**e6_groups**: the changed kernel with PV in four groups at 4.20, 4.45, 4.641 and 4.70. **e8_novs_groups**: the same without VS (as in e3_novs, that part is left out).

```
-    "PV": 4.641,
+    "PV": (4.2, 4.45, 4.641, 4.7),
```

> The changed kernel with its own table, PV in four groups of 16 at 4.20, 4.45, 4.641, 4.70 (the last two next to each other), no waits between. F: stalls within PV fall from 239 us to about half or less, and with them the time at half clock (642 us); 4000 to 4180. If it stays at 4250 although the stalls fall, the time goes elsewhere (waits of TensorE for banks, as in the split run with the old table).

> Both at once: no transfers of VS (PV reads VV in its place, the even query blocks get the wrong keys) and PV in four groups. F and C together: stalls within PV under 60 us, time below the 3980 of the run without VS, 3800 to 3920. What is left above 3834 would be the copy on GpSimd, the four transfers of PP and the new table.

4299.6 and 4076.5 us, 47 and 96 more than with PV whole, where 4000 to 4180 and 3800 to 3920 had been expected. The stops by issue fell from 239 to 62.9 + 66.2 = 129 us in the first, as forecast, but not the time at the half level, and three more entries per m at 0.39 us (m1_bursts) are by estimate up to 192 x 3 x 0.39 = 225 us of TensorE's time, more than was to be had.

No version that I ran is faster than the kernel before.

## Why the prediction was wrong

**What PV costs with the change: the rate right, the price wrong.** "I take 15 ns again: 128 x 0.015 = 1.9 us" is what the timeline shows, eight records per 0.12 us. Neither the loads in turn (21 ns or more) nor S1's 10 ns came. The Trainium skill, "TensorE: Matmul & The Clock Gate", section "Part 3: Packing small matmuls — row/col tiling", lets a weight load overlap matmuls in flight only where its row group is another one, and its section "Wait — 56ns, not 53.3ns?" puts no less than about 25 ns between starts. The timeline disagrees with both for pieces side by side: two column pieces on the same 64 rows go on together, and starts stand 15 ns apart. But PV's price per m, with the idle time in it, is 719.5 / 192 = 3.75 us, and not 2.05; before it was 614.1 / 192 = 3.20. The sum's term of minus 131 us (and 36 for the waits ahead of it) came out as plus 105. The step that failed is that a rate read from runs of 32 records was taken for a run of 128 close behind another run of 128. What it lacked is that the instructions must have come by then: 256 of them arrive with one packet of q8, one per 3.7 us in the long runs of m2_forms, and 236.5 us of stops in PV end just behind the landing of such a packet. That the rival of loads in turn had the same 3.75 us per m is chance: its sign, 21 ns per record or more, isn't there.

**"TensorE would be busy less and the clock stays as it is": wrong, 229 us.** TensorE's other work takes 229 us more, with 485 us more at the half level. The clock goes with TensorE's idle time, which rose by 255 us where the forecast had it 21 lower: every fall counted in the six layers stands behind some, near and far keep nearly the full clock, and the old form loses it just as well in f3_stop, f4_vs and f5_vs_apart. In e3_novs (327 us), e7_vschunks (457) and e10_warm (371) stops and half level fall together. How much the form adds isn't settled.

**Traffic, costed at nothing: 273 us.** Its amount was near (94 MB as forecast, 9 points more of the DMA engines where 7 were, 7.0 and 8.5 us to landing where 5 to 9 was the estimate, and PV doesn't wait for it). What was asked was only if the data come in time. e3_novs against the changed kernel gives 273 us, f1_split_novs against e1_split 179, for data that nobody waited for. The ways that I can show: instructions later (m1_bursts, compact form 11% slower under traffic; in the changed kernel 39% of the packets that ended a stop in PV had transfers of q10, VS's queue, beside them, of all packets 24%) and the clock behind the stops. ScalarE's issues are 192 x 0.65 = 125 us of its time, as forecast (70 to 125), and f4_vs shows what such issues do when seven stand in a row; how the 273 us divide between traffic and issues stays open.

**One run in place of four, costed as a gain: a loss.** e4_bmerged has the place alone, in the old form and with its waits between the groups: plus 300 us, by copies of V and by the layer's end that become late. The changed kernel's own table avoids much of that (58 us ahead of XCH, as before), and then pays in PV.

**GpSimd's copy and the longer chain.** The copy takes 1.04 us, inside the bounds, and is free where nobody waits for it (b2_copy). The room of 1.34 steps was enough: PV waits 6.5 us for PX in the changed kernel. f3_stop shows what the old place would have paid: 287 us. RB's wait fell from 727 to 261 us as forecast, and it was worth nothing, which b3_rb says too (485 us, ratio 1.0022).

**The waits.** TensorE's for VectorE fell to 50 us where I let them grow to 96; VectorE waits for TensorE by way of ScalarE instead (SX, 692 us where it was 89 in the kernel before). The rival "swallowed by new waits" had the right symptom, more than 290 us of idle time, with the wrong engine: in the page it is TensorE itself, by issue, and PV isn't at its 2.1 us.

What isn't settled: the effects don't add. Table, form, traffic and chain each cost 140 to 300 us when put in or taken out alone, and the whole costs 414. e1_split has 193 us less of stops in PV than the changed kernel and the same time. That an instruction packet is what a stop inside PV waits for is read from the times of the packets; no row names it. Why the packet comes late, how the traffic delays it, and what ScalarE's issues add were not separated by any run.

## What to carry to other kernels

Small products have two prices: what one costs in its run, and how many instructions in a row the engine can be given. Before many short ones are merged into one run, look at what stands next to it and count instructions per us over some microseconds; 256 in 3.7 us was the most that came here in a long run. Where TensorE is at 93%, count a new stop at more than its own length: here the clock was at its half level for a while behind many of them, and slowed the wide products there. And a DMA is not free because its data come in time: price the issue on its engine (0.53 to 0.66 us here) and, by a run without it, what its traffic does to the others.

## What the hardware showed that I had not expected

- TensorE's instructions come in packets of 256 that land 3.66 to 3.68 us apart in long runs of small products. Of 152 stops in PV of the changed kernel, 151 end 1.15 to 1.75 us behind such a landing.
- In a stream of products of 64 rows by 32 columns the granted clock fell to its half level behind a stop of 1.33 us, and stayed there with TensorE busy; with four wide products behind each 64 it kept 1.00. More work took less time: 56.8 us against 63.4.
- Stops of another origin do the same to the old form: 738 us at the half level in f5_vs_apart, with 717 us of idle time.
- Each change from wide products to small ones and back costs 0.39 to 0.41 us beside the products themselves.
- VS's transfers at a DMA share of 0.40 slow a TensorE that reads none of their data: 139.9 us against 126.2.
- GpSimd's one-input copy of 128x1024 takes 1.04 us, its two-input operation of the same size 1.91.
